# First layer of a two-layer decoder: two groups of sequences in flight instead of one

## What is computed

```python
x = x + L0_attn(layernorm(x))             # stage A
x = x + L0_xattn(layernorm(x), ctx, ctx)  # stage B
x = x + L0_ffn(layernorm(x))              # stages C and D, then the experts
# A: q = tanh(x Wc + b); shell = normalised x Ws + b; proj = shell omega + bias
#    phi = combine(powers of q  x  [cos, sin](proj))
#    out = softmax(phi phi^T * decay + causal) (x Wv + b) Wo + b
# B: softmax(q k^T) v over the 361 context rows, then * Wv
# C: h = layernorm(x); 16-head causal self attention of h; y = h + attn Wo + b
# D: scores = layernorm(y) gate_w; the two best of 8 experts per token
```

## Time and profile before

| | |
|---|---|
| median of three runs | 1757.67 us |
| the profiled execution's own time | 1750.97 us |
| its span, first to last instruction | 1749.3 us |
| mean granted TensorE clock | 0.845 |
| busy in the span | PE 74%, DVE 57%, ACT 29%, POOL 24% |
| first layer up to the gate scores of group 3 | 24 to 613.3 us |
| of this, group 1 | 163.3 to 313.3 us |

### The profile page before, as it was taken

The page is one execution under the profiler, slowest core; times in us unless marked ns, Lnnn a source line. Parts: engine busy times, 40 slices in busy tenths (PEclk is TensorE's granted clock), DMA queues, the critical chain, the costliest instruction groups (busy, mean ns, idle before and its releaser), DMA issues.

```text
span 1749.3 us, 24353 instructions
## 1 busy us (share of the span) xinstructions
PE 1288.6 (74%) x7936; PEld 903.6 (52%) x7936; DVE 989.1 (57%) x2088; ACT 505.2 (29%) x1201; POOL 411.9 (24%) x528
## 2 busy tenths in 40 slices
PE   2676677577666759998145988859888598885988
PEld 1554464355445436665123765437654476554865
DVE  4446526535453623332577777667676676766852
ACT  2222223122122312221012642226412263232630
POOL 1032125116212420000662111221113221132100
PEclk9687679578667969999567998969999699997998
DMA  9410010009200321110131421015210152102501
GB/s 375 171 44 1 1 44 20 1 24 394 101 0 19 141 101 49 43 48 28 45 111 44 104 67 38 11 43 110 61 39 11 43 118 52 39 10 61 122 14 47
DMA packets 69685, 122.28 MB, mean 70 GB/s; under 512 B 25404, under 2 KB 55100, under 8 KB 68032
## 3 DMA queue, kind: packets, MB, share of 16 engines
q1 hardware_dynamic: 63936, 110.04, 21.1%
q0 software_dynamic: 5632, 10.77, 2.2%
HBM read 67.69 MB, written 53.07 MB: 69 GB/s over the span
## 4 chain that ended last, share of the span: by engine, by line
issue 50%; PE 26%; POOL 11%; DVE 5%; POOLq 4%; ACT 2%; DMA 1%; DVEq 1%; SPq 0%; ACTq 0%
PE ps L1022 6%; PE ps L1041 3%; PE ps L1269 3%; POOL headbd L634 3%; PE ps L547 2%; POOL experts L1574 2%; PE ps L490 1%; PE ps L482 1%; PE ps L1195 1%; POOLq L1591 1%; POOL xn L533 1%; POOL small L439 1%; DVE probs L589 1%; POOL tok_d L1546 1%; POOL x L1520 1%
## 5 line engine op out<-in xcount | busy, mean ns | idle before, releaser
L1474 ACT ACTIVATE probs<-ps,small 100x361 f32<-100x361 f32 x256 | 141.5, 558 | 93.5 <-DVE small L2086 89.0
L464 PE MATMUL ps<-cst,xn 100*128 100x100 f32 x256 | 50.9, 352 | 120.3 <-DVE xn L428 82.1
L634 POOL TENSOR_TENSOR headbd<-kT,cst 128x800 f32<-128x800 f32 x64 | 97.5, 1527 | 164.5 <-DVE kT L1976 100.0
L2086 DVE TENSOR_REDUCE small<-ps 100x2 f32<-100x722 f32 x128 | 115.6, 906 | 35.6 <-PE ps L1181 35.6
L547 PE MATMUL ps<-headbd,qT 128*100 128x400 f32 x256 | 113.3, 524 | 21.5 <-POOL headbd L634 21.5
L1022 PE MATMUL ps<-every,xT_t 128*128 x256 | 122.3, 601 | 0.4 <-issue 0.4
L1269 PE MATMUL ps<-hT,experts 128*128 128x400 f32 x288 | 114.1, 546 | 1.2 <-DVE small L667 1.2
L1195 PE MATMUL ps<-cst,probs 100*121 100x100 f32 x768 | 104.0, 271 | 8.2 <-DVE probsT L2094 7.7
L464 PEld LDWEIGHTS ps<-cst,xn 100*128 100x128 f32 x256 | 35.8, 198 | 138.0 <-DVE xn L428 83.8
L1195 PEld LDWEIGHTS ps<-cst,probs 100*121 100x121 f32 x768 | 94.7, 185 | 22.7 <-issue 14.3
L611 ACT ACTIVATE probs<-probs 100x800 f32<-100x800 f32 x64 | 55.7, 870 | 170.6 <-DVE probs L589 170.6
(11 more groups left out here) (303 smaller groups left out, 2719.3 us busy)
## 6 DMA issues: line engine op xcount, KB each, us to landing
k_stack<-key_d SPq DMA_DIRECT2D x192, 90.5 KB, 3.2
tok_d<-wt SPq DMA_DIRECT2D x1, 14848.0 KB
res_d<-wt SPq DMA_DIRECT2D x1, 14848.0 KB
every<-e_d SPq DMA_DIRECT2D x8, 1536.0 KB, 18.4
ctxT<-ctxT_d SPq DMA_DIRECT2D x8, 726.0 KB, 5.3
key_d<-k_hi SPq DMA_DIRECT2D x32, 181.0 KB, 3.0
key_d<-k_lo SPq DMA_DIRECT2D x32, 181.0 KB, 3.4
gates<-gate_d SPq DMA_DIRECT2D x28, 200.0 KB, 4.4
```

The source lines that it names most:

```text
L464: ins = e.transpose(part(b0)[:, c, i * S:(i + 1) * S], src[:, b, c * P:(c + 1) * P], identS)
L634: inc(e.tensor_tensor(headbd[:, u % 2], keysT[:, c, b * S:(b + 1) * S].unsqueeze(1).broadcast_to([P, HC, S]), cs("head").unsqueeze(2).broa ...
L1474: ins = e.activation(f_e[:, n % 2, i, 0:LC], bank(2 * (n % 2) + i, S, LC), ACT.Exp, bias=h_nm[:, n % 2, i:i + 1], accum_out=h_sum[:, b, h: ...
L2086: inc(e.tensor_reduce(h_nm[:, n % 2, 0:2], ps[0:S, 2 * (n % 2):2 * (n % 2) + 2, 0:LC], AX, ALU.max, negate=True), "F_nm")
```

## The change

The front chains (A and B) of group g+1 now run in the same stretch of the program as the projections, self attention, output projection, D norm and router of group g. `early(g, h)` holds the 17 PE steps of A and B, `behind(g)` everything after them. `woven` puts them together in a fixed order of 18 rounds.

```diff
+ROUNDS, STEPS = 18, 19
+def woven(x0, x1, y):
+    for _ in range(ROUNDS):
+        for st in (x0, y, x1, y):
+            next(st)
...
-            in_turn(before_c(0, 0), before_c(0, 1))
-            from_c(0)
-            with e.Fori(1, NG) as g:
-                in_turn(before_c(g, 0), before_c(g, 1), ahead(g - 1))
-                from_c(g)
-            list(ahead(NG - 1))
+            in_turn(early(0, 0), early(0, 1))
+            woven(early(1, 0), early(1, 1), behind(0, False))
+            with e.Fori(1, NG - 1) as g:
+                woven(early(g + 1, 0), early(g + 1, 1), behind(g, True))
+            list(behind(NG - 1, True))
+            ahead(NG - 1)
```

```diff
+            def attend(g):
+                def scores(m):
+                    b, c, q = step_of(m)
+                    W(e, "C_bd", g, m // 2 + 1)
+                    if m >= 2:
+                        W(e, "C_sub", g, m - 1)
+                    o = bank(4 + m % 2, S, 4 * S)
...
+                for n in range(STEPS):
+                    if n < 16:
+                        scores(n)
+                    if 2 <= n <= 17:
+                        turn(n - 2)
+                    if n >= 3:
+                        values(n - 3)
+                    yield
...
+            def attend(g):
+                def shift(m):
+                    W(e, "C_s", g, m + 1)
+                    sc = bank(4 + m % 2, S, 4 * S).rearrange("p (h n) -> p h n", h=4)
+                    nm = h_nm[:, m % 2, 0:4]
+                    e.tensor_reduce(nm, sc, AX, ALU.max)
+                    e.drain()
+                    if m >= 4:
+                        W(e, "C_pTp", g, m - 3)
+                    inc(e.tensor_tensor(quad(probs, m).rearrange("p (h n) -> p h n", h=4), sc,
+                                        nm.unsqueeze(2).broadcast_to([S, 4, S]), ALU.subtract), "C_sub")
...
+            def attend(g):
+                for n in range(STEPS):
+                    if n < 16:
+                        W(e, "C_sub", g, n + 1)
+                        inc(e.activation(quad(probs, n), quad(probs, n), ACT.Exp), "C_e")
+                    if 2 <= n <= 17:
+                        m = n - 2
+                        W(e, "C_pTp", g, m + 1)
...
+                        inc(e.activation(quad(probsT, m), bank(6, S, 4 * S), ACT.Copy), "C_pT")
```

`early` gets its own buffers for the norm, hT, qT and the transposed probabilities (`xnX`, `hTX`, `qTX`, `pTX`), in the place of the third expert's weights, which are loaded later for that; the C norm gets statistics of its own. `early` leaves its x in `xall`, where `behind` takes it from. SP loads x when A_xb, ctxT when B_s and ctxk when B_oTp of both halves are done:

```diff
             with e.Fori(0, NG - 1) as g:
+                W(e, "A_xb", g, 1, 1)
+                e.dma_start(xin[:], x_d[g + 1]).then_inc(ld["x"].sem, 16)
+                W(e, "B_s", g, 1, 1)
+                e.dma_start(ctxT[:], ctxT_d[g + 1]).then_inc(ld["ctxT"].sem, 16)
                 W(e, "B_oTp", g, 1, 1)
-                load_group(g + 1)
+                e.dma_start(ctxk, ctx_d[g + 1]).then_inc(ld["ctxk"].sem, 16)
```

More of the change, by code:

```diff
@@ L1381, in _ @@
+            in_turn(early(0, 0), early(0, 1))
+            woven(early(1, 0), early(1, 1), behind(0))
+            with e.Fori(1, NG - 1) as g:
+                woven(early(g + 1, 0), early(g + 1, 1), behind(g))
+            list(behind(NG - 1))
             e.wait_ge(r_tiles.sem, 1)
@@ L1791, in after_c, with behind @@
+            def behind(g, routed):
+                ways = route(g - 1) if routed else iter(())
+                group = xall[:, bass.ds(g * NB, NB), :]
+                norms = [norm_dve(e, "C_", g, h, group, y) for h in range(2)]
+                next(norms[0])
+                next(ways, None)
                 yield
[L1792 to L1793 removed]
+                next(norms[1])
                 yield
[L1795 removed]
@@ new lines, in behind @@
+                for h in range(2):
+                    W(e, "C_vp", g, 1, h)
+                    inc(e.tensor_scalar(c_v[:, own(h), :], tokens(5 + 2 * h), 1.0, None, ALU.mult), "C_v")
+                    yield
+                yield
+                yield from attend(g)
+                yield
+                yield
+                for h in range(2):
+                    W(e, "C_rT", g, 1, h)
+                    W(e, "C_oT", g, h + 1)
+                    inc(e.tensor_tensor(qT[:, :, tok(h)], oT[:, :, tok(h)], hT[:, :, tok(h)], ALU.mult), "C_yT")
+                    yield
@@ new lines, in behind @@
+                norms = [norm_dve(e, "D_", g, h, y, xd) for h in range(2)]
+                for h in range(2):
+                    W(e, "C_out", g, 1, h)
+                    W(e, "C_xb", g, 1, h)
+                    add_out(y, 5 + 2 * h, h)
+                    next(norms[h])
+                    yield
+                for h in range(2):
+                    if h == 0 and routed:
+                        e.wait_ge(r_sent.sem, g * (2 * NB * 16))
+                    inc((yield from norms[h]), "D_xn")
+                    e.tensor_tensor(xall[:, bass.ds(g * NB + HB * h, HB), :], group[:, own(h), :], y[:, own(h), :],
+                                    ALU.add)
+                    e.drain()
+                    yield
@@ L1804, in route @@
+                for h in range(2):
+                    scores_dve(e, "D_", g, h, g_s[:, own(h), :], 5 + 2 * h)
+                    yield
             def route(g):
-                yield
                 e.drain()
```

479 lines of the change are left out of this document (319 added, 160 removed).

## The result

The changed kernel takes 1689.13 us, the median of 4 runs (1686.5 to 1699.07), against 1754.58 for the kernel before beside it. The ratio is 0.9637, 95% interval 0.9587 to 0.9687: faster by 3.6%. Forecast were 1696 us, range 1645 to 1745. The profiled run took 1689.45 us with a span of 1687.8, so the span is 61.5 us shorter, nearly the 61 of the sum. It is not the sum that I wrote, though: the first layer gave 71.9, and the second took 10.4 back.

A forecast was written before the change was run, and what follows sets the result against it. The first layer was taken as bound by latency, PE, DVE and ACT waiting in a ring. Weaving two groups cuts it from 613.3 to 552 us, 61 less: 1690 by the profiled execution, 1696 as median, range 1645 to 1745.

The forecast's parts named there:

- the sum: First layer: start, group 0's front, three passes, group 3's rest and loop jump make 552 us against 613.3, 61 us less.
- A pass of 126 us, the first 122: First layer: one woven pass takes 126 us, against 150 in turn; the first has no router and takes 122.
- The rounds: The pass's 18 rounds, each as long as its fullest engine or longer where PE and DVE alternate; sum 127 us.
- the ring of the D norm: Rounds 15 to 17: PE 13.4 us, DVE 9.0, with the D norm's waits between engines 15.5 us.
- ACT just fits, so I add nothing: Round 4: four table loads, sines, exponentials and copies take ACT 8 us in a round of 9; nothing added.
- The second layer is untouched: After the first layer: costed at nothing; the stretch from the first layer's end on stays as long as before.
- The 6.7 us that I added for the median: Whole kernel: the median of runs stands 6.7 us above the profiled execution, turning 1690 into 1696 us.
- The signs: Profile checks: first layer ends near 552 us, pass 120 to 132, clock above 0.8, self attention some 75 us long.
- Taking turns: Rival, whole pass: PE and DVE alternate throughout, pass over 146 us; at 155 the time is 1783 us; chance 0.11.
- no change: Rival, whole pass: finer steps cost what the weave gives; pass 143 to 149 us, time 1747 to 1765; chance 0.07.
- deep overlap: Rival, whole pass: the chains cover each other nearly fully, pass near 100 us, time 1618 us; chance 0.10.
- Twice the time for a table load: Rival, round 4: four loads at 2.6 us make it 13.3 us instead of 9, time 1709 us; chance 0.04.

The follow-up runs named there:

- e1: The changed kernel with the weave taken out, front chains and the rest of the other group in turn: 1761.43 us, ratio to the kernel before 1.004.
- e2: The changed kernel with tanh in place of the front chain's sine, so no table load is left in a pass; one run: 1713.67 us.
- e6: The same kernel as e2 (tanh for the sine in the changed kernel), measured again: median 1693.84 us, ratio to the kernel before 0.9692.
- e9: The changed kernel with 64 small memsets on VectorE between two drains, ahead of the second layer's loop; one run: 1690.5 us.
- e10: The changed kernel with 128 small memsets on VectorE ahead of the second layer's loop; one run: 1690.0 us.
- e11: The changed kernel with VectorE's C_yT one step earlier and 128 memsets ahead of the second layer's loop: 1681.39 us, ratio to the kernel before 0.958.

## Why the prediction was right

- **What bounds it, and the mechanism: right.** e1 shows that the overlap is all of the gain. The work of a pass was foreseen as PE 98.5 and DVE 76.7 us; the third pass holds 93.7 and 76.9.
- **A pass of 126 us, the first 122: right,** 123.0, 123.2 and 126.0. The rest of group 3 took 77.2 for 78. The 3 us for the loop's jump do not show. The front of group 0 took 68 for 73: my row of before had 11 more instructions on DVE, the next stage's. Together 541.4 for 552. The fill of res_d, costed at nothing, met rounds 0 to 3 of the third pass (DMA 1.01): the same steps took 32.9 us there and 31.7 in the second pass, so it cost some 1.2 us.
- **The rounds: right in kind, off in size.** Three pairs came within 1.1 us (17.9 for 19, 13.9 for 14, 16.5 for 15.5). Rounds 0 and 1 took 17.6 for 15, 4 and 5 took 20.2 for 18, 6 to 8 took 18.0 for 14.5; rounds 9 and 10 took 12.8 for 15.6, and 15 to 17 took 9.1 for 15.5. Rounds 9 and 10 are short by the clock: I took PE's 9.1 us from a row at 0.61, and 1.00 was granted; 9.1 x 0.61 + 6.4 is 12.0, and PE was busy for 12.8. In rounds 15 to 17 the clock (0.92, for rows at 0.73 and 0.71) explains about 3 of the 6.4 us, and the 2.1 that I added for the ring of the D norm did not show (PE was busy for 8.95 of 9.1 us); the other 1.5 I can't place. I gave the clock 4 us back in one lump, where it had to be given round by round. In rounds 4 to 8 both engines wait for each other more than I allowed. The errors add up to -1.1 us: the sum was lucky in its parts.
- **"ACT just fits, so I add nothing": wrong as read, right in effect.** ACT is busy for 8.8 of the 20.2 us of rounds 4 and 5, but its order makes PE wait 5.03 us, and 4.5 and 2.2 with no load left (e2, e6). Without any load the total is the same within the measurement (e6).
- **"The second layer is untouched": this step failed.** The code is the same, the time is 10.4 us more: 7.9 in the two self attentions behind the loop's jump, where DVE stalls for 6 us and PE's clock falls from 1.00 to 0.89, and 2.8 in the last stretch, at 0.87 for 0.90. The two self attentions grew with DVE's stall, which is already there in the unwoven e1 (5.98 and 5.99 us); why the last stretch runs at a lower clock is open. It was hidden in the total because the first layer gave 10.9 us more than forecast. That the profiled time met the sum within 1 us (1689.45 for 1690) is luck: two errors of over 10 us cancelled. The 6.7 us that I added for the median did not come either (1689.13 against 1689.45), and they are nearly the whole distance of the forecast from the result.
- **The signs.** PE's largest wait in rounds 4 to 10 is for ACT's probsT, not for DVE's subtraction or POOL's keys; PE waits for DVE in rounds 11 to 14 as foreseen. The self attention of a pass was to be some 75 us long; in the third pass it runs from 372.7 to 438.6, 66 us, which is about what my own rounds add up to.
- **The clock above 0.8 in a pass: right** (0.83 to 0.85). PE's busy time in the first layer fell by 14.2 us; I had counted 12 for the three passes.
- **The rivals.** Taking turns, no change and deep overlap are all out: a pass would have been over 146, 143 to 149 or near 100. Twice the time for a table load is out by the timeline.

What stays open: what decides whether a stretch gets 1.2 or 2.4 GHz. One kernel got either in the same place (e2 and e6); the edits of the first layer went with the lower level more often, and none brought the higher one.

## What to carry to other kernels

Two dependent chains on one engine pair are worth weaving even where the engines look three quarters busy: add up each engine's work per stage, take the fuller one, and reckon its duration at both levels of the clock, because that moves too: here PE's work of one row at 0.61 ran at 1.00, and self attention at 0.97 became 0.85 to 0.89. Below one per cent, do not rank edits by one run or by the wait they remove: PE's idle time fell and its busy time rose in every edit of the woven first layer here. And if code that jumps stands behind what is changed, its time can move though nothing in it does.

## What the runs showed of the hardware that was not expected

- The granted clock fell behind a stretch in which PE was the busier: 6.89 of 8 us busy, then 0.53; in the other run of the kernel 5.75 of 8, then 1.00 (e2 and e6).
- DVE stood still for 5.94 to 6.03 us behind a loop's jump in ten executions, and for 3.1 to 4.7 when its code had been moved by 64 or 128 instructions (e9, e10, e11).
- A table load on ACT took 1.28 us and, before exponentials, nothing around it: 0.02 us before and 0.01 after.
- A DVE instruction on 64x200 elements took 0.26 us alone and 1.55 when POOL's 128x800 had started 0.08 us ahead of it.
